# Filling the start of a transformer kernel: eight constant matmuls up to the first patches, first rows scaled ahead of a weight split, second half's rows turned one product sooner

## What is computed

```
x = einsum('bchpwq,dcpq->bhwd', patches, patch_w) + patch_b
x = layernorm(x, ln_g, ln_b) + sinusoidal_pe
identity = x
x = ff(x); x = sparse_attn(x) + identity      # ff: gelu(y @ ff1 + b1) @ ff2 + b2
x = ff(x) + identity
h = concat([x, txt]); h = h + attn(layernorm(h)); h = h + experts(layernorm(h))
```

## Time and profile before

| | us |
|---|---|
| median of 3 runs | 225.53 |
| lowest, highest | 224.13, 226.31 |
| the profiled execution, its time | 226.03 |
| the profiled execution, its span | 224.2 |
| TensorE busy | 212.6 |
| VectorE busy | 151.0 |

### The profile page before, as it was taken

One profiled execution on the slowest core, in us unless ns is written; L12 is line 12 of the kernel. 1 busy time (PEld: TensorE's weight loads), 2 busy tenths in 40 slices (PEclk: granted clock), 3 DMA queues, 4 the chain that ended last, 5 costly groups with the idle time before them and its releaser, 6 DMA issues.

```text
span 224.2 us, 4277 instructions
## 1 busy us (share of the span) xinstructions
PE 212.6 (95%) x1438; PEld 192.4 (86%) x1438; DVE 151.0 (67%) x406; ACT 112.9 (50%) x227; POOL 35.3 (16%) x61
## 2 busy tenths in 40 slices
PE   6989999999999998999898999999999999999992
PEld 2979998886899986785877897999999999999991
DVE  0168986899204465665769499698878787878763
ACT  2228855557752734431214576266655555555542
POOL 8011003543920524040004000000000000000000
PEclk9999999999999999999999999999999999999999
DMA  6997000000000000021000000655554544544303
GB/s 224 406 394 215 0 1 4 0 3 0 4 0 0 0 3 0 0 61 37 0 3 0 0 18 20 180 154 161 175 140 145 177 141 142 135 135 135 88 0 105
DMA packets 10225, 19.09 MB, mean 85 GB/s; under 512 B 1441, under 2 KB 4657, under 8 KB 10210
## 3 DMA queue, kind: packets, MB, share of 16 engines
q1 hardware_dynamic: 9632, 17.35, 24.7%
q10 hardware_dynamic: 578, 1.54, 1.9%
HBM read 18.25 MB, written 0.64 MB: 84 GB/s over the span
## 4 chain that ended last, share of the span: by engine, by line
PE 76%; DVE 15%; issue 2%; ACT 2%; DMA 2%; POOL 1%; DVEq 0%
PE bank L530 6%; PE bank L532 6%; PE bank L531 6%; PE bank L533 6%; PE bank L534 6%; PE bank L578 4%; PE bank L567 3%; PE bank L1018 3%; PE bank L690 3%; PE bank L1028 2%; PE bank L1019 2%; PE bank L1024 2%; PE bank L1020 2%; PE bank L648 2%; DMA patches<-in_patches 2%
## 5 line engine op out<-in xcount | busy, mean ns | idle before, releaser
L1342 ACT ACTIVATE hid_s<-hid 128x384 fp32r<-128x384 f32 x34 | 17.8, 525 | 28.1 <-DVE hid L1784 27.8
L1332 ACT ACTIVATE silu<-bank,expert_raw 128x384 f32<-128x384 f32 x34 | 19.6, 578 | 9.9 <-PE bank L534 9.7
L1766 DVE SCALAR_TENSOR_TENSOR gated<-bank,expert_raw,silu 128x384 f32<-128x384 f32 x32 | 19.6, 614 | 7.0 <-PE bank L534 6.6
L1790 DVE TENSOR_TENSOR hid_s<-hid,hid_s 128x384 fp32r<-128x384 f32 x34 | 18.6, 553 | 8.4 <-ACT hid_s L1342 8.3
L530 PE MATMUL bank<-tA,ug_w 128*128 128x384 f32 x68 | 23.1, 340 | 0.1
L533 PE MATMUL bank<-tB,ug_w 128*128 128x384 f32 x68 | 22.9, 337 | 0.0
L532 PE MATMUL bank<-tA,ug_w 128*128 128x384 f32 x68 | 22.9, 337 | 0.0
L531 PE MATMUL bank<-tA,ug_w 128*128 128x384 f32 x68 | 22.9, 337 | 0.0
L534 PE MATMUL bank<-tB,ug_w 128*128 128x384 f32 x68 | 22.9, 336 | 0.0
L567 PE MATMUL bank<-filler 128*128 128x512 bf16 x50 | 16.8, 412 | 1.3 <-POOL table L426 1.3
L1784 DVE TENSOR_TENSOR hid<-w_all,gated 128x384 f32<-128x384 f32 x30 | 16.5, 553 | 1.8 <-issue 1.7
(11 more groups left out here) (332 smaller groups left out, 541.5 us busy)
## 6 DMA issues: line engine op xcount, KB each, us to landing
w_all<-routing_weights SPq DMA_DIRECT2D x15, 384.0 KB, 3.7
expert_raw<-in_experts SPq DMA_DIRECT2D x17, 256.0 KB, 3.7
expert_raw<-in_experts SPq DMA_DIRECT2D x17, 97.0 KB, 1.9
patches<-in_patches SPq DMA_DIRECT2D x3, 384.0 KB, 7.4
ff_raw<-in_ff ACTq DMA_DIRECT2D x1, 768.0 KB, 7.4
kv_raw<-in_kv SPq DMA_DIRECT2D x1, 578.0 KB, 11.9
patch_w<-in_patch_w ACTq DMA_DIRECT2D x2, 288.0 KB, 4.0
ff_raw<-in_ff SPq DMA_DIRECT2D x1, 576.0 KB, 8.7
```

What stands on the lines that cost most here:

```text
L1332: a(silu[hf][:, :], bank[3 + 2 * hf][:, 0:H2N], ACT.Silu, bias=expert_raw[:, p, BU:BU + 1]).then_inc(s[f"silu{hf}"], 1)
L1342: a(hid_s[p][:, 0, H2N * hf:H2N * hf + H2N], hid[hf][:, :], ACT.Copy)\
L1766: v.scalar_tensor_tensor((hid if first else gated)[hf][:, :], bank[4 + 2 * hf][:, 0:H2N], expert_raw[:, p, BG:BG + 1], silu[hf][:, :], ALU ...
L1790: v.tensor_tensor(hid_s[p][:, 1, tok], hid[hf][:, :], f(hid_s[p][:, 0, tok]), ALU.subtract)\
```

## The change

There are three edits:

1. The memset of `filler` moves from GpSimd to VectorE, as its first instruction, and TensorE waits for that. TensorE runs eight fillers instead of six ahead of the patches. The two fillers ahead of `hidden1(0)` and the one ahead of `hidden1(1)` go.
2. VectorE scales half 0's rows ahead of the first half of ff1's remainder instead of behind it. The waits for ff1 and its rounded part stay ahead of both.
3. `turn_x(x, 1)` comes after four products of half 0 instead of five, on TensorE and ScalarE. VectorE makes the remainders of half 1's turned rows ahead of `bqm` instead of behind it.

```diff
 FILL = {
-    "patches": 6, "turn_x0": 0, "hidden0": 2, "turn_x1": 0, "hidden1": 1, ...
+    "patches": 8, "turn_x0": 0, "hidden0": 0, "turn_x1": 0, "hidden1": 0, ...
@@ GpSimd
-            g.memset(filler[:, :], 1.0).then_inc(s["filler_done"], 1)
             g.memset(table[:, :], 0.0).then_inc(s["filler_done"], 1)
@@ TensorE
-            pe.wait_ge(s["filler_done"], 1)
+            pe.wait_ge(s["vec_step"], 1)
             keep_busy("patches", bank[7])
-            pe.wait_ge(s["filler_done"], 5)
+            pe.wait_ge(s["filler_done"], 4)
             patch(0)
...
-            hidden1(0, range(0, 5))
+            hidden1(0, range(0, 4))
             keep_busy("turn_x1", bank[6])
             turn_x(x, 1, "x_done", bank[6], bank[7])
-            hidden1(0, range(5, FK))
+            hidden1(0, range(4, FK))
@@ ScalarE
-            gelu(0, (1, 2, 3), "hid1_ps", "gelu_done", range(0, 5))
+            gelu(0, (1, 2, 3), "hid1_ps", "gelu_done", range(0, 4))
             turned_hi(1, 2, bank[6], bank[7])
-            gelu(0, (1, 2, 3), "hid1_ps", "gelu_done", range(5, FK))
+            gelu(0, (1, 2, 3), "hid1_ps", "gelu_done", range(4, FK))
@@ VectorE
             step, after = chain(dve, "vec_step")
+            step(v.memset(filler[:, :], 1.0))
...
             dve.wait_ge(d_ff1, 16)
             dve.wait_ge(s["ff1_hi"], 1)
+            token_scale(0, k)
             ff1_lo(slice(0, FF // 2), "ff1_lo")
-            token_scale(0, k)
             dve.wait_ge(s["ff1_hi"], 2)
             ff1_lo(slice(FF // 2, FF), "ff1_lo")
...
+            turned_lo(1, 2, bank[6], bank[7])
             dve.wait_ge(d_cols, 32)
             for ch in range(2):
                 v.tensor_scalar(bqm[:, ch, :], ...)
-            turned_lo(1, 2, bank[6], bank[7])
```

More of the change, by code:

```diff
@@ L1185, in load_table @@
             def load_table(function, k):
-                act.wait_ge(s["filler_done"], 2)
+                act.wait_ge(s["filler_done"], 1)
                 a(table[0:1, k:k + 1], table[0:1, k:k + 1], function)
@@ L1194, in _ @@
             act.dma_start(const[:, 0:CONST_FIRST], d["const"][:, 0:CONST_FIRST]).then_inc(d_const, 16)
-            act.wait_ge(s["filler_done"], 5)
+            act.wait_ge(s["filler_done"], 4)
             act.dma_start(rows[0:1, 0:ROWS_FIRST], d["rows"][:, 0:ROWS_FIRST]).then_inc(d_rows, 16)
```

## The result

The changed kernel takes 223.66 us (median of 20 runs, 223.06 to 224.56) against 225.69 us (20 runs, 224.13 to 227.52): 0.9919 of it, 95% interval 0.9898 to 0.9939, so 1.8 us faster by this ratio; the two medians themselves lie 2.0 us apart. The profiled execution took 223.08 us with a span of 221.3.

What follows compares the result with a forecast made beforehand. TensorE bounds the kernel (76% of the span), with a low clock until about 9.4 us and an idle wait on VectorE's chain. Start 1.6 plus edits 2 and 3 0.8 is 2.4 us, from 225.53 to 223.1 us, range 222.2 to 225.1.

Steps and rivals of the forecast that it cites:

- Edit 1, the pause and its cost: TensorE ahead of the patches: eight fillers remove the 0.65 us pause; patches start at about 4.8 us, 0.1 us paid.
- Edit 1, the clock: TensorE at the start: unpaused work raises the clock at 6.0 us instead of 9.4, net 1.6 us, bounds -0.1 to 2.2.
- Edit 2: VectorE after block 1: scaling starts at 14.25 us instead of 14.74, transposes 0.5 us earlier; 0.8 us together with edit 3.
- Edit 3: Half 1: turned remainder starts at 22.0 us instead of 22.81, fourth matmul at 23.0 instead of 23.83; 0.8 us with edit 2.
- The first rival: TensorE's start: the clock rises no earlier, only the turns gain; 224.8 us, chance 0.18.

Runs made afterwards that it cites:

- twelve fillers: The changed kernel with twelve fillers ahead of the patches instead of eight: 224.20 us, 0.9955 of before.
- no start fillers: The changed kernel with no fillers ahead of the patches: 225.62 us, 1.0002 of before.
- six fillers: The changed kernel with six fillers ahead of the patches instead of eight: 224.27 us, 0.9952 of before.
- before again: The kernel before, unchanged, run once for a second profile: 223.98 us.
- eight on GpSimd: The kernel before with eight fillers instead of six ahead of the patches, memset still on GpSimd: 224.38 us, 0.9967 of before.
- start alone: The kernel before with the memset on VectorE and eight fillers ahead of the patches, all else as before: 224.49 us, 0.9973 of before.
- scaling alone: The kernel before with edit 2 only, half 0's rows scaled ahead of ff1's first remainder half: 224.55 us, 0.9990 of before.
- turn alone: The kernel before with edit 3 only, half 1 turned after four products and its remainders ahead of `bqm`: 224.59 us, 0.9991 of before.
- turns alone: The kernel before with edits 2 and 3 and without the three later fillers, start as before: 225.59 us, 0.9985 of before.
- changed again: The changed kernel, unchanged, run and profiled again in a later group: 223.90 us, 0.9931 of before.

## Why the prediction was right, and where it was off

Forecast 223.1, measured 223.66, inside the range of 222.2 to 225.1. The outcome "within 1% of before", where 0.9919 lies, had a chance of 0.54. The direction and the mechanism of edits 2 and 3 were right; the clock's term was mis-sized, and its account of the pause is not borne out.

- **Edit 1, the pause and its cost: nearly right.** No idle ahead of the patches, which start at 4.61, and at 4.85 in the second profile. With six fillers they started at 4.71 in two profiles but at 4.39 to 4.60 in four others, so in some runs eight, which end at 4.85 at the lower rate, can cost up to 0.5 us, not 0.1. The loads that the forecast looked at bound nothing; the small load of the rows, which it left out, did (last section). The memset's length was right (0.48 for 0.52), its start not: 0.92 instead of 0.74.
- **Edit 1, the clock: mis-sized.** "It now rises at 6.0 us instead of 9.4 ... net 1.6 us" took the one late rise of the profile for the kernel's habit. The starts close up at 4.3 us in the changed kernel's profile and at 5.8 in its second. In the pair of profiles the mark moved by even more than 1.6, 2.0 us. But five of the six profiles with six fillers, the second of the kernel before among them, have the clock up in spite of the pause: that the pause kept it down, as the forecast had it, is not shown. So over many runs the start is worth 1.8 - 0.9 = 0.9 us, and 0.6 and 0.7 us where it was tried alone (1.0 and 1.1 by the medians). Against the late kind the forecast is nearer: 226.03 less its 2.4 is 223.6, and the changed kernel's median is 223.66; that they agree this well is luck, for the profiled pair lies 2.95 us apart. The mistake was to carry 1.6 us over to the median of 225.53, the middle of three runs of which one, at 224.13, was of the other kind.
- **The page's rule** (the Trainium skill, "TensorE: Matmul & The Clock Gate", Part 1) that the ramp differs from run to run and should not be fitted would have been the better guide. The two profiles of the kernel before bear it out. Its size, under 1% of a typical span, is about met. With the clock up from the patches on, the mark comes 5.45 us behind their start (twelve fillers, 6.55 and 12.00); it came 7.60 us behind it with no start fillers and 7.81 in the first profile of before. That is 2.2 and 2.4 us lost, 1.0% and 1.1% of the span.
- **A miscount without effect.** From 4.71 to 9.32 us the kernel before has 15 starts and 14 distances, not 14 starts; the 0.33 us stands.
- **Edit 2: right.** Scaling directly behind the root, transposes 2.70 us after the mark (forecast 2.6), 0.4 us at half 1's remainder and at the end, alone.
- **Edit 3: right.** Forecast 10.5 us from the mark to the fourth matmul, measured 10.41. TensorE's idle time ahead of the transposes is 0.23 us and not 0.5, because half 0's product started 0.1 us later than forecast and the drain of its last matmul covers part of it. Edits 2 and 3 gave 0.9 us for 0.8, and it lasted to the end.
- **The first rival** (the clock rises no earlier) is true of those runs, 52 in 116 if the times are read as two kinds, in which it had already risen early. The forecast saw it as one case or the other for the kernel; it is a mixture of runs.

What stays open: why the same program with the same timeline finds the clock up in one run and not in the other. No kernel here could set it. Nor is it shown whether two more fillers help by filling the pause or by lengthening the work.

## What to carry to other kernels

A profile shows one run. Where the clock's rise lies near the start, look at the spread of the times before pricing it: a single profile here was off the median of its first three runs by 0.5 us and off the better half of the runs by 2. In this kernel it paid to fill the wait for the first load with matmuls, but not beyond it: two more made the spread of the times narrower and the times 0.7 us shorter, four more on top lost 0.5 to 0.8. A reordering that is hidden in the spread of the times can be read from a mark in the trace that lies behind the uncertain part, best at an instruction close behind the reordering: the fourth matmul of half 1's first product stood at 10.40 or 10.41 us with no start fillers and with six fillers as in the changed kernel, while the whole span behind the mark was off by 1.7 and 0.6 us in these two profiles.

## What the runs showed that was not expected

- The page's granted clock reads 1.00 also where matmuls run at half the rate (the earlier trace rows and the 4.18 us for block 0 in the run with no start fillers). The starts of the matmuls are what tells.
- With the clock up early, block 0's bias matmul waits for its row, a load that the forecast did not look at. Where nothing holds it, it starts 0.16 us behind the last patch matmul (twelve fillers, before again). In the changed kernel it is 0.26 us, with eight on GpSimd 0.33, with six fillers 0.36, in the start alone 0.44; the matmul before is still draining, so the timeline shows no idle time there, but the view of the line does. In the start alone (`--source L580`, 4 to 9.3 us), what its engine sat idle for:

```profile
  DMA rows<-in_rows: 0.4, 1
```

  In the scaling alone, the turn alone and the turns alone the wait is 0.38, 0.58 and 0.76 us even behind the drain. In the turns alone:

```profile
7.71 0.59 PE L581 MATMUL bank<-rows,kv_w 128*128 128x192 f32 x2 [0.76 <-DMA rows<-in_rows]
```

  So in seven of the fourteen profiles this load, and not TensorE's clock, sets when block 0 ends. It is issued once GpSimd has zeroed the rows, at 2.39 us before and at 2.15 to 2.18 with the memset moved. The wait is there with either and absent with either (before again, changed again), so the issue time alone does not decide it; an earlier load was not tried.
